# Ten of twenty zeroing transfers move from the GpSimd queue to the sync queue

## The chip, the cores and the metric

The kernel runs on one NeuronCore of one Trainium2 chip. The metric is the device time of one execution in microseconds (us); the kernel before has a median of 4244.83 us over three runs (4243.64 to 4254.43).

## The reference

Two layers of a graph network over 6250 nodes of width 256 and 106250 edges, sorted by destination, each followed by a residual and a layer norm.

```python
edge_index = jnp.stack([src, dst])
# layer 0: a message per edge, summed over the edges of node ei
hi, hj = h[ei], h[ej]
x = jnp.concatenate((hi, hj, d2), axis=-1)
msg = silu(x @ mW1 + mb1)
msg = layer_norm(msg, ln_g, ln_b)
msg = silu(msg @ mW2 + mb2)
agg = segment_sum(msg, ei, num_segments=6250)
y = silu(concatenate((h, agg)) @ uW1 + ub1) @ uW2 + ub2
x = layernorm(x + (h + y))
# layer 1: gather, mean by node, one linear layer
agg = segment_sum(x[src], dst) / maximum(counts, 1)
x = layernorm(x + relu(agg @ W.T + b))
```

## The kernel before

The 6250 nodes are 50 blocks of 125. The edges are 832 tiles of 128, handled four at a time: 208 quads (and 220 quads of "visits", since a tile that lies over two blocks is visited twice). The first matrix of the message is applied to the nodes, not to the edges, so that an edge's input is a sum of two rows: one of a table P in HBM (`p_tab`), gathered by the edge's index, and one of a table Q that stays in SBUF (`big`), spread over the edges by a one-hot matmul.

The stages, in the times of the profile:

- 0 to about 142 us: P is computed block by block and stored, while the index tables are made. SP issues the stores (line 480), the two tables of places and edge weights (lines 460, 462), and other transfers.
- 142 to about 195 us: Q is computed (line 787 on TensorE, 1013 and 1016 on ScalarE, 1419 and 1423 on VectorE). On GpSimd the gathers of P begin at 148 us (`gather_0`, line 628). The ring in SBUF (`ring0`) holds 16 quads of gathered rows.
- From 202 us the expansion: for each quad v SP loads its places (line 450, 125 KB from `loc_tab`) and its weights (line 452, 3 KB) in `place_rows(v)`; VectorE makes the one-hot matrix of it (line 1445); TensorE multiplies it with Q (line 836); VectorE adds the product onto the gathered rows (line 1464). The places have two buffers, so `place_rows(v)` waits on SP for the expansion of quad v-2 (semaphore `qexp`). On VectorE the order is: add quad v, one-hot of quad v+2, add quad v+1. The expansion runs 14 quads ahead of the message: the first SiLU (line 1034, ScalarE) waits until quads 0 to 13 are added.
- From 282 to 2896 us the messages: SiLU, norm, second matrix, SiLU, and a matmul that joins edges of a tile with the same node. Then GpSimd adds the 128 rows of each tile onto one of four tables of sums in HBM (`sums`, line 639, an accumulating indirect DMA). GpSimd gathers quad g+16 only once the SiLU of quad g has read its place in the ring (line 625), and adds quad q once ScalarE has written its sums (line 634). After the 16 gathers that fill the ring, each quad costs GpSimd four gathers and four adds.
- 2896 to 3092 us: the nodes of layer 0 (the four tables are read, added and multiplied). From 3092 us on: layer 1, with gathers of its own.

The four tables of sums, 6400 rows each, must be zero before the first add. `zero_piece(eng, i)` (line 397, its DMA at line 401) writes one fifth of one table: 1280 KB from an SBUF tile of zeros, which is `scr`, the tile that VectorE's `count_before` (line 1509) writes later, and so waits for all twenty pieces (line 1504). In the kernel before GpSimd issues all twenty: pieces 0 to 9 during the P stage, each after five more blocks, and pieces 10 to 19 one behind each of the first ten quads of gathers (line 648). `weight_rows(part)` on SP (line 468) copies weight rows into Q; part 2 waits for the last matmul of Q (`s_qmm`), and TensorE's first expansion waits for it (line 869).

The order on every queue is the order of the code: each engine's block is written out, and SP's `message_loop` (line 491) comes right after `weight_rows(2)`.

Of the kernel before, what the change touches and what calls it, by code (L numbers as in the profile page):

```python
# [27 lines left out]
BLOCKS = N // NB  # L28
# [5 lines left out]
TABLES = QT  # L34
# [4 lines left out]
XGROUP = 5  # L39
# [8 lines left out]
LAG = -(-BEHIND // QT) + 1  # L48
# [5 lines left out]
def gnn(nc, x, src, dst, edge_w, mW1, mb1, ln_g, ln_b, mW2, mb2, uW1, ub1, uW2, ub2, W, b, out):  # L54
# [13 lines left out]
    with ExitStack() as ctx:  # L68
        def sb(name, shape, dt=f32):
            return ctx.enter_context(nc.sbuf_tensor(name, shape, dt))  # L70

        def sem(name):
            return ctx.enter_context(nc.semaphore(name))
# [36 lines left out]
        cnt = sb("cnt", [NB, 2, BLOCKS])  # L110
# [8 lines left out]
        def cut(shape, dt=f32, parts=P):  # L119

            n = 1
            for m in shape:
                n *= m
            words = n if dt != bf16 else n // 2
            ap = arena[:, at_[0]:at_[0] + words]
            at_[0] += words
            assert at_[0] <= at_[1], at_
            ap = ap if dt == f32 else ap.bitcast(dt)
            names = "abcd"[:len(shape)]
            ap = ap.rearrange(f"p ({' '.join(names)}) -> p {' '.join(names)}", **dict(zip(names, shape)))  # L130
            return ap[0:parts]
# [47 lines left out]
        half = cut([2, 2, D])  # L179
        agg = cut([2, D])  # L180
        col = cut([2, 2 * H, P])
        xin = cut([2, D])
        hpre = cut([2, D])
        hpre2 = cut([2, D])
        hid = cut([2, D])
# [23 lines left out]
        mom = sb("mom", [P, 2, 5, QT])  # L209
# [34 lines left out]
        def by_place(rows_, group):  # L244
# [2 lines left out]


        s_const, s_constc, s_zeroed, s_pad = sem("s_const"), sem("s_constc"), sem("s_zeroed"), sem("s_pad")
        s_edges, s_weights, s_tables = sem("s_edges"), sem("s_weights"), sem("s_tables")  # L250
        s_ends, s_tile, s_prev, s_range = sem("s_ends"), sem("s_tile"), sem("s_prev"), sem("s_range")
        s_epart, s_blk, s_pick, s_picked, s_visit = (sem("s_epart"), sem("s_blk"), sem("s_pick"), sem("s_picked"),
                                                     sem("s_visit"))
# [24 lines left out]
                ["hot", "agg", "acc"]]  # L278
        e = [{n: sem(f"e{l}_{n}") for n in EDGE[l]} for l in range(2)]

        BLOCK = ["load0", "load1", "xcopy", "half", "agg", "cnt", "cols", "colev", "hmm", "hpre", "hid", "hcols", "hcolev",
                 "omm", "oadd", "res", "stat", "mom", "newt", "norm"]
        k = [{n: sem(f"b{l}_{n}") for n in BLOCK} for l in range(2)]
        s_scaled, s_lastnorm = sem("s_scaled"), sem("s_lastnorm")
        s_mean, s_biased, s_shift = sem("s_mean"), sem("s_biased"), sem("s_shift")
        s_norm1 = {n: sem(f"s_norm1_{n}") for n in ("dve", "act")}
# [77 lines left out]
        def later(q, n):  # L364

            return not isinstance(q, int) or q >= n
# [24 lines left out]
        def load_x(eng, g):  # L391
            rows_ = x[g * XGROUP * NB:(g + 1) * XGROUP * NB, :].rearrange("(j p) d -> p j d", p=NB)
            for a, z in SPLIT:
                eng.dma_start(pxin[a:z, g % 2, :, :], rows_[a:z]).then_inc(s_xload[g % 2], 16)
        ZPIECES = 5

        def zero_piece(eng, i):
            rows_ = SUMROWS // P * D // ZW
            n, a = rows_ // ZPIECES, i % ZPIECES * (rows_ // ZPIECES)
            whole = sums[i // ZPIECES].rearrange("(p a b) d -> p a (b d)", p=P, a=rows_)  # L400
            eng.dma_start(whole[:, a:a + n, :], zeros[:, :].unsqueeze(1).to_broadcast([P, n, ZW]))\
                .then_inc(s_tables, 16)

        def visit_blocks(eng, q, regs):

# [10 lines left out]
        def _(sp):  # L416
# [47 lines left out]
            def weight_rows(part):  # L464
                a, z, done = W_PARTS[part]
                if done:
                    sp.wait_ge(s_qmm, done)
                sp.dma_start(big[NB:P, a:z, :, :].rearrange("p j k d -> p j (k d)"),
                             w1cp[0:PARTS, :, :].rearrange("p k d -> p (k d)").unsqueeze(1)
                             .to_broadcast([PARTS, z - a, PARTS * D])).then_inc(s_wrow, 16)  # L470
# [12 lines left out]
                place_rows(v, v)  # L483
            for part in range(1, len(W_PARTS)):
                weight_rows(part)


            def step_0(q, k_):
# [70 lines left out]
        def _(pool):  # L559
# [46 lines left out]
                    pool.sem_inc(s_turn_pool, 1)  # L606
                    place(c)

            EARLY = BLOCKS // XGROUP
            for i in range(EARLY):  # L610
                pool.wait_ge(s_xt, XGROUP * (i + 1))
                zero_piece(pool, i)
            pool.wait_ge(s_padrows, 16 * 2)
            for par in (0, 1):
                pool.wait_ge(s_pst[par], 32 * ((BLOCKS // PAIR + 1 - par) // 2))
# [5 lines left out]
            def gather_0(g):  # L621
                if g >= RING_QUADS + 4:
                    pool.wait_ge(e[0]["pre"], QT * (g - 3))
                if g >= RING_QUADS:
                    pool.wait_ge(e[0]["silu"], 2 * (g - RING_QUADS + 1))
                for u in range(QT):
                    tile = g * QT + u
                    pool.indirect_dma_start(  # L628
                        out=ring0[:, tile % RING, :], out_offset=None, in_=p_tab[:, :],
                        in_offset=bass.IndirectOffsetOnAxis(ap=esrc[:, tile:tile + 1], axis=0))\  # L630
                        .then_inc(landed(g)[0], 16)

            def add(q, par):
                pool.wait_ge(e[0]["tot"], q + 1)
                pool.wait_ge(e[0]["sidx"], q + 1)
                for u in range(QT):
                    if q >= 1:
                        pool.wait_ge(e[0][f"added{u}"], q * 16)
                    pool.indirect_dma_start(  # L639
                        out=sums[u][:, :], in_=tot[:, par, u, :], in_offset=None,  # L640
                        out_offset=bass.IndirectOffsetOnAxis(ap=sidx[:, par, u:u + 1], axis=0),
                        compute_op=ALU.add).then_inc(e[0][f"added{u}"], 16)

            for q in range(-LAG - 1, TILE_QUADS + 2):
                if q + LAG + 1 < TILE_QUADS:
                    gather_0(q + LAG + 1)
                if q + LAG + 1 < TABLES * ZPIECES - EARLY:
                    zero_piece(pool, EARLY + q + LAG + 1)
                if q == 2:
                    pool.wait_ge(s_tables, 16 * TABLES * ZPIECES)  # L650
                if q >= 2:
                    add(q - 2, q % 2)

# [8 lines left out]
                                      .rearrange("p a d -> p (a d)")).then_inc(k[0]["xcopy"], 1)  # L662
            steps(pool, BLOCKS, 0, copy_x)
            pool.wait_ge(s_x1st, STORES)
            pool.wait_ge(s_tables, 16 * TABLES * ZPIECES)
            pool.wait_ge(s_esrc, 1)
            for tile in range(TILE_QUADS * QT):

# [503 lines left out]
        def _(dve):  # L1172
# [327 lines left out]
            def count_before(q, par, u):  # L1500

                if u == 0:
                    if isinstance(q, int) and q == 0:
                        dve.wait_ge(s_tables, 16 * TABLES * ZPIECES)
                        dve.wait_ge(s_padrows, 16 * 2)
                    dve.wait_ge(s["same"], q + 1)
                    if later(q, 1):
                        dve.wait_ge(s["dup"], QT * q)
                nc.vector.tensor_tensor_reduce(out=scr[:, u, :], in0=same[:, par, u, :], in1=lower[:, :],
                                               scale=1.0, scalar=0.0, op0=ALU.mult, op1=ALU.add,  # L1510
                                               accum_out=dup[:, par, u:u + 1]).then_inc(s["dup"], 1)
# [21 lines left out]
            def step_0(q, k_):  # L1533
                par = k_ % 2
                o = 1 - par

                def beside(i):
                    if live(q - 1, TILE_QUADS):
                        if i == 0:
                            sum_rows(q - 1, o, 0)  # L1540
                        elif i == 1:
                            count_before(q - 1, o, 0)
                            count_before(q - 1, o, 1)
                        elif 8 < i <= 10:
                            count_before(q - 1, o, i - 7)
                        elif i == 12:
                            sum_rows(q - 1, o, 1)
                        elif i == 14:
                            sum_rows(q - 1, o, 2)
                    if live(q + LAG + 2, QUADS) and i == 4:  # L1550
                        one_hot(q + LAG + 2, (k_ + LAG) % 2)
                if live(q + LAG, QUADS):
                    add_in(q + LAG, (k_ + LAG) % 4)
                if live(q, TILE_QUADS):
                    stage_keys(q, par)
                    norm(q, par, beside)
                else:
                    for i in range(5 + 2 + 3 * NEWTON):
                        beside(i)
# [207 lines left out]
```

## Time and profile before

| what | value |
|---|---|
| median of three runs | 4244.83 us (4243.64 to 4254.43) |
| span of the profiled execution, first to last instruction | 4447.1 us |
| busy share of the span: TensorE, VectorE, ScalarE, GpSimd | 73%, 61%, 34%, 68% |
| DMA queue q0 (software, GpSimd's) | 353.53 MB, 41.7% of 16 engines |
| DMA queue q1 (hardware, SP's) | 93.80 MB, 7.4% |
| granted TensorE clock, mean | 0.858 |

The span is the profiled execution's own time as far as the profile gives it: 202 us longer than the median of the runs that were timed without a profile. Of an instruction on a DMA-issuing queue a row tells when it was issued and how long the issue took; when its bytes landed is told apart.

### The profile page before, as it was taken

Reading aid. Unit: us, or ns where it says so; the run is one execution under the profiler, and the core shown is the slowest. Engines: PE = TensorE matmul, PEld = TensorE weight load, DVE = VectorE, ACT = ScalarE, POOL = GpSimd, SP = SyncE. Lnnn points to the kernel's source line nnn. Section 1 sums busy time; section 2 is a strip of 40 time slices with the busy share of each in tenths; the row PEclk is TensorE's granted clock in tenths of the full one; section 3 lists DMA queues with packets and bytes.
Section 4 is the critical chain, followed back from the end, with each engine's and each line's share of the span. In section 5 each row is a group of like instructions: output and inputs, shape, how many; then the busy total and the mean of one; then the engine's idle time right before and its main releaser. Section 6 shows DMA issues by size and latency. Waiting matters only on the chain. (4 is left out here: it accounts for less than half of the span.)

```text
span 4447.1 us, 77452 instructions
## 1 busy us (share of the span) xinstructions
PE 3267.0 (73%) x16199; PEld 2413.6 (54%) x16200; DVE 2708.1 (61%) x12039; ACT 1491.9 (34%) x2782; POOL 3024.4 (68%) x2641
## 2 busy tenths in 40 slices
PE   6757777777777777777777778887476766667676
PEld 4446666566666666665666666675243433334345
DVE  5456666666666666666666667777344444444457
ACT  1324444444544444444444445633000000000005
POOL 1538888888888888888888887612666666666643
PEclk9878998889899899899998989998777777777788
DMA  6725555555555555555555555755333333333323
GB/s 194 257 67 93 93 94 94 93 94 95 93 93 94 94 92 94 94 93 93 94 94 92 94 94 85 132 158 161 90 92 90 90 90 92 90 91 91 90 61 113
DMA packets 315268, 455.28 MB, mean 102 GB/s; under 512 B 51945, under 2 KB 255301, under 8 KB 314949
## 3 DMA queue, kind: packets, MB, share of 16 engines
q0 software_dynamic: 206400, 353.53, 41.7%
q1 hardware_dynamic: 103317, 93.80, 7.4%
q10 hardware_dynamic: 5232, 5.12, 0.4%
q14 instruction: 293, 2.40, 0.2%
q8 instruction: 26, 0.43, 0.0%
HBM read 296.41 MB, written 155.62 MB: 102 GB/s over the span
## 5 line engine op out<-in xcount | busy, mean ns | idle before, releaser
L639 POOL DMA_INDIRECT sum<-arena,sidx x832 | 1321.3, 1588 | 294.2 <-issue 254.1
L671 POOL DMA_INDIRECT arena<-x_tab,esrc x832 | 796.5, 957 | 436.9 <-issue 188.7
L945 PE MATMUL ps<-arena 128*125 x1760 | 711.4, 494 | 444.5 <-DVE arena L1703 217.8
L628 POOL DMA_INDIRECT arena<-p_tab,esrc x832 | 820.7, 986 | 309.5 <-issue 246.5
L812 PE MATMUL ps<-arena 128*128 128x256 f32 x1664 | 560.5, 496 | 444.5 <-ACT arena L1062 442.7
L849 PE MATMUL ps<-w,arena 128*128 128x256 f32 x3328 | 833.6, 383 | 3.9 <-ACT arena L1072 3.9
L945 PEld LDWEIGHTS ps<-arena 128*125 128x125 f32 x1760 | 392.6, 241 | 744.0 <-issue 681.9
L1703 DVE TENSOR_TENSOR arena<-ps,arena 125x257 f32 x880 | 374.7, 426 | 647.7 <-remote 219.5
L812 PEld LDWEIGHTS ps<-arena 128*128 128x128 f32 x1664 | 389.9, 246 | 550.3 <-issue 485.1
L849 PEld LDWEIGHTS ps<-w,arena 128*128 128x128 f32 x3328 | 567.4, 190 | 121.0 <-issue 4.7
L1464 DVE TENSOR_TENSOR arena<-ps,arena 128x256 f32 x880 | 373.0, 424 | 381.5 <-issue 197.8
L1044 ACT ACTIVATE arena<-ps,key 128x128 f32<-128x128 f32 x832 | 237.8, 369 | 1090.1 <-remote 1076.9
L836 PE MATMUL ps<-arena 128*128 x2640 | 411.6, 317 | 53.3 <-DVE arena L1464 27.0
L1473 DVE BATCH_NORM_STATS2 bst<-arena 128x6 f32<-128x256 f32 x832 | 312.4, 417 | 226.9 <-ACT arena L1034 224.2
L1144 ACT ACTIVATE arena<-ps 128x250 f32<-128x250 f32 x50 | 18.8, 376 | 1250.6 <-PE ps L965 1249.5
L836 PEld LDWEIGHTS ps<-arena 128*128 128x128 bf16 x2640 | 304.5, 115 | 174.2 <-issue 86.2
L949 PE MATMUL ps<-identh 128*128 128x512 bf16 x832 | 387.9, 466 | 0.0
L1496 DVE TENSOR_SCALAR arena<-arena,mom,nwt 128x256 f32<-128x256 f32 x832 | 313.0, 437 | 37.1 <-DVE nwt L387 30.2
L822 PE MATMUL ps<-ident,arena 128*128 128x128 f32 x1664 | 225.9, 279 | 132.8 <-DVE arena L1496 90.5
L1055 ACT ACTIVATE arena<-ps,gb 128x512 f32<-128x512 f32 x416 | 320.4, 770 | 8.2 <-PE ps L822 6.0
L822 PEld LDWEIGHTS ps<-ident,arena 128*128 128x128 f32 x1664 | 185.4, 143 | 188.4 <-DVE arena L1496 93.7
L1072 ACT ACTIVATE arena<-ps 128x1024 f32<-128x1024 f32 x208 | 213.1, 1024 | 166.3 <-PE ps L812 76.5
(189 smaller groups left out, 4049.1 us busy)
## 6 DMA issues: line engine op xcount, KB each, us to landing
arena<-loc_tab SPq DMA_DIRECT2D x220, 125.0 KB
sum<-scr POOLq DMA_DIRECT2D x20, 1280.0 KB
arena<-sum SPq DMA_DIRECT2D x200, 128.0 KB, 2.2
arena<-p_tab,esrc POOLq DMA_INDIRECT x832
sum<-arena,sidx POOLq DMA_INDIRECT x832
arena<-x_tab,esrc POOLq DMA_INDIRECT x832
arena<-x_tab SPq DMA_DIRECT2D x50, 128.0 KB, 2.0
p_tab<-arena SPq DMA_DIRECT2D x25, 224.0 KB
```

The source lines that it names most:

```text
L628: pool.indirect_dma_start(out=ring0[:, tile % RING, :], out_offset=None, in_=p_tab[:, :], in_offset=bass.IndirectOffsetOnAxis(ap=esrc[:, t ...
L639: pool.indirect_dma_start(out=sums[u][:, :], in_=tot[:, par, u, :], in_offset=None, out_offset=bass.IndirectOffsetOnAxis(ap=sidx[:, par, u ...
L671: pool.indirect_dma_start(out=ring[:, tile % LATER_RING, 0:D], out_offset=None, in_=x1_tab[:, :], in_offset=bass.IndirectOffsetOnAxis(ap=e ...
L812: last = nc.tensor.matmul(ps[:, PM + u // 2, u % 2 * D:(u % 2 + 1) * D], same[:, par, u, :], msg[:, par, u, 0:D], start=True, stop=True)
L822: last = nc.tensor.transpose(ps[:, PZ + h, u * P:(u + 1) * P], act[:, par, u, h * P:(h + 1) * P], ident[:, :])
L836: last = nc.tensor.matmul(ps[:, PP + u // 2, u % 2 * D:(u % 2 + 1) * D], hott[:, par, u, :], big[:, bass.ds(blocks_[u], 1), i, :].rearrang ...
L849: nc.tensor.matmul(to, zt[:, par, h, u * P:(u + 1) * P], w2[:, h, :], start=h == 0, stop=False)
L945: nc.tensor.matmul(ps[0:NB, u, 0:CW], same1[:, par, u, :], ring[:, bass.ds(at[u], 1), :].rearrange("p a c -> p (a c)"), start=True, stop=T ...
L949: nc.tensor.matmul(ps[:, PK, :], identh[:, :], identh[:, :].unsqueeze(1).to_broadcast([P, QT, P]), start=True, stop=True)
L1055: nc.scalar.activation(zt[:, par, h, :], ps[:, PZ + h, :], ACT.Identity, bias=gb[:, h, 1:2], scale=gb[:, h, 0:1]).then_inc(s["zev"], 1)
L1464: nc.vector.tensor_tensor(row, ps[:, PP + u // 2, u % 2 * D:(u % 2 + 1) * D], row, ALU.add)\
L1703: nc.vector.tensor_tensor(row, ps[0:NB, u, 0:CW], row, ALU.add).then_inc(s["acc"], 1)
```

## The change

SP issues pieces 10 to 19, in one run after `weight_rows(2)` and ahead of its message loop, on a semaphore of their own (`s_later`). GpSimd no longer issues them between gathers. The waits for zeroed tables now ask both semaphores, and GpSimd's second wait, ahead of the gathers of layer 1, is left out. Some semaphores that nothing used are no longer made.

```diff
+        EARLY = BLOCKS // XGROUP
-        def zero_piece(eng, i):
+        def zero_piece(eng, i, zeroed):
...
-                .then_inc(s_tables, 16)
+                .then_inc(zeroed, 16)
...
             for part in range(1, len(W_PARTS)):
                 weight_rows(part)
+            for i in range(EARLY, TABLES * ZPIECES):
+                zero_piece(sp, i, s_later)
...
             for q in range(-LAG - 1, TILE_QUADS + 2):
                 if q + LAG + 1 < TILE_QUADS:
                     gather_0(q + LAG + 1)
-                if q + LAG + 1 < TABLES * ZPIECES - EARLY:
-                    zero_piece(pool, EARLY + q + LAG + 1)
                 if q == 2:
-                    pool.wait_ge(s_tables, 16 * TABLES * ZPIECES)
+                    pool.wait_ge(s_tables, 16 * EARLY)
+                    pool.wait_ge(s_later, 16 * (TABLES * ZPIECES - EARLY))
...
             pool.wait_ge(s_x1st, STORES)
-            pool.wait_ge(s_tables, 16 * TABLES * ZPIECES)
...
-                        dve.wait_ge(s_tables, 16 * TABLES * ZPIECES)
+                        dve.wait_ge(s_tables, 16 * EARLY)
+                        dve.wait_ge(s_later, 16 * (TABLES * ZPIECES - EARLY))
```

## Rows read from the trace of the kernel before

**Rows 1.** The waits of the whole span: who waited for whom, total, times, longest.
```profile
POOL sum L639 <- issue: 254.1, 802, 6.6
POOL arena L628 <- issue: 246.5, 809, 0.3
POOL arena L628 <- ACT arena L1034: 49.8, 2, 45.1
```
**Rows 2.** Timeline of GpSimd: start, duration, engine, line, operation, idle time before.
```profile
148.47 1.15 POOL L628 DMA_INDIRECT arena<-p_tab,esrc  x1 [7.08 <-DMA p_tab<-arena]
...
153.65 0.92 POOL L401 DMA_DIRECT2D sum<-scr  x1
...
208.75 0.92 POOL L401 DMA_DIRECT2D sum<-scr  x1
...
237.56 0.95 POOL L628 DMA_INDIRECT arena<-p_tab,esrc  x1 [0.30 <-issue]
238.81 0.95 POOL L628 DMA_INDIRECT arena<-p_tab,esrc  x1 [0.30 <-issue]
284.85 0.95 POOL L628 DMA_INDIRECT arena<-p_tab,esrc  x1 [45.09 <-ACT arena L1034]
...
305.75 1.64 POOL L639 DMA_INDIRECT sum<-arena,sidx  x1 [6.60 <-issue]
```
**Rows 3.** Timeline of ScalarE: the table load ahead of the first SiLU.
```profile
282.14 1.28 ACT L1034 ACT_TABLE_LOAD   x1 [87.10 <-DVE arena L1464]
```
**Rows 4.** Timeline of VectorE during the expansion of the first quads.
```profile
212.20 0.35 DVE L1445 TENSOR_SCALAR arena<-arena,tnum 125x512 bf16<-125x512 bf16 x1 [5.75 <-DMA arena<-loc_tab]
...
220.98 0.35 DVE L1445 TENSOR_SCALAR arena<-arena,tnum 125x512 bf16<-125x512 bf16 x1 [2.58 <-issue]
224.23 0.42 DVE L1464 TENSOR_TENSOR arena<-ps,arena 128x256 f32 x1 [2.90 <-issue]
...
237.47 0.42 DVE L1464 TENSOR_TENSOR arena<-ps,arena 128x256 f32 x1 [12.24 <-remote]
...
243.95 0.42 DVE L1464 TENSOR_TENSOR arena<-ps,arena 128x256 f32 x1 [2.88 <-remote]
...
247.15 0.35 DVE L1445 TENSOR_SCALAR arena<-arena,tnum 125x512 bf16<-125x512 bf16 x1 [0.96 <-DMA arena<-loc_tab]
...
278.93 0.35 DVE L1445 TENSOR_SCALAR arena<-arena,tnum 125x512 bf16<-125x512 bf16 x1 [1.85 <-PE ps L836]
```
**Rows 5.** Timeline of SP's queue, from the last two weight row copies on.
```profile
168.14 26.38 SPq L468 DMA_DIRECT2D arena<-arena  x2
205.28 0.28 SPq L450 DMA_DIRECT2D arena<-loc_tab  x1
```
**Rows 6.** Windows: busy us of each engine, granted clock, DMA share, GB/s.
```profile
180.00:190.00 10.00, 9.66 (x41) 6.40 (x40) 7.38 (x20) 6.58 (x21) 7.87 (x9) 1.00 0.93 325
195.00:215.00 20.00, 5.25 (x27) 3.33 (x28) 4.28 (x11) 0.04 (x1) 15.74 (x17) 0.61 0.93 303
230.00:240.00 10.00, 1.38 (x6) 0.77 (x6) 0.85 (x2) 0.00 (x0) 7.59 (x8) 0.50 0.40 114
```
**Rows 7.** DMA issues of the page: size of each.
```profile
arena<-loc_tab SPq DMA_DIRECT2D x220, 125.0 KB
sum<-scr POOLq DMA_DIRECT2D x20, 1280.0 KB
```
**Rows 8.** Timeline of SP's queue late in layer 1: a store, then small loads.
```profile
4391.70 1.04 SPq L513 DMA_DIRECT2D out_dram<-arena  x2
4392.78 19.69 SPq L543 DMA_DIRECT2D arena<-x_tab  x10
```
**Rows 9.** Line 543 from 4392 to 4396 us, then the page's row of such loads.
```profile
DMA to landing us min/median/max: 6.3/6.3/6.3
...
arena<-x_tab SPq DMA_DIRECT2D x50, 128.0 KB, 2.0
```
**Rows 10.** SP's queue as it loads x, and the DMA queues from 2842 to 2845 us.
```profile
2839.74 27.39 SPq L496 DMA_DIRECT2D arena<-in_x_dram  x10
...
q1 hardware_dynamic: 847, 0.87, 108.6%
```

More of the change, by code:

```diff
@@ L249, in gnn @@
         s_const, s_constc, s_zeroed, s_pad = sem("s_const"), sem("s_constc"), sem("s_zeroed"), sem("s_pad")
-        s_edges, s_weights, s_tables = sem("s_edges"), sem("s_weights"), sem("s_tables")
+        s_edges, s_weights, s_tables, s_later = sem("s_edges"), sem("s_weights"), sem("s_tables"), sem("s_later")
         s_ends, s_tile, s_prev, s_range = sem("s_ends"), sem("s_tile"), sem("s_prev"), sem("s_range")
@@ L279, in gnn @@
         e = [{n: sem(f"e{l}_{n}") for n in EDGE[l]} for l in range(2)]
-        BLOCK = ["load0", "load1", "xcopy", "half", "agg", "cnt", "cols", "colev", "hmm", "hpre", "hid", "hcols", "hcolev",
-                 "omm", "oadd", "res", "stat", "mom", "newt", "norm"]
-        k = [{n: sem(f"b{l}_{n}") for n in BLOCK} for l in range(2)]
+        BLOCK = [["load0", "load1", "xcopy", "half", "agg", "cols", "colev", "hmm", "hpre", "hid", "hcols", "hcolev",
+                  "omm", "oadd", "res", "stat", "mom", "newt", "norm"],
+                 ["load0", "load1", "cnt", "cols", "colev", "omm", "res", "stat", "mom", "newt"]]
+        k = [{n: sem(f"b{l}_{n}") for n in BLOCK[l]} for l in range(2)]
         s_scaled, s_lastnorm = sem("s_scaled"), sem("s_lastnorm")
@@ L607, in _ @@
                     place(c)
-            EARLY = BLOCKS // XGROUP
             for i in range(EARLY):
                 pool.wait_ge(s_xt, XGROUP * (i + 1))
-                zero_piece(pool, i)
+                zero_piece(pool, i, s_tables)
             pool.wait_ge(s_padrows, 16 * 2)
```

## The prediction

> **What bounds the kernel now.** I read the total waits first. From the first add on, GpSimd waits for almost nothing but its own issue: 254.1 us of 0.3 us gaps before adds, 246.5 us before gathers, and one long wait of 45.1 us, for the first SiLU [rows 1]. So over most of the span, 306 to 2896 us, GpSimd sets the pace, and what happens before moves the end only as far as it moves the moment at which that chain starts: the first SiLU at 282.14 us [rows 3], after which the seventeenth quad is gathered at 284.85 and the first add is issued at 305.75 [rows 2]. Second, the timelines from 148 us to there. GpSimd fills its ring by 239.8 and then stands idle for 45.09 us [rows 2]; it is early. ScalarE had waited 87.10 us for VectorE's adds [rows 3]. The late chain is the expansion: places from SP's queue, one-hot, matmul, add, quad by quad [rows 4]. It starts when part 2 of the weight rows has landed and then needs the places of quads 2 to 13. VectorE's one-hot of quad 2 comes at 212.20, released by that small load, which SP issued at 205.28 [rows 4, 5]: 6.9 us for 125 KB, at a time at which the DMA engines were 0.93 busy at 303 GB/s [rows 6].
>
> **The change part by part.**
>
> GpSimd loses ten issues of 0.92 us, the first at 153.65, the last at 208.75 [rows 2]: 9.2 us. Its ring would be full at 230.6 rather than 239.8. What hides this gain is the 45.09 us of waiting right behind it, so it is worth nothing; it would be worth 9.2 us only if the first SiLU came before GpSimd was done.
>
> SP gains ten issues at 194.5, where the last weight row copy ends (168.14 + 26.38) [rows 5]. All of SP's later instructions stand behind them: place_rows(2), (3) and all that follow, and so VectorE's one-hot of quad 2, everything behind that on VectorE in order (the add of quad 1, the one-hot of quad 3), TensorE's expansion of quad 2 and the first SiLU. Quads 0 and 1 are not touched; their places were loaded before.
>
> What these ten cost in the queue is not shown by the trace of before for these transfers, but a close case is: near the end SP issues a store of 1250 KB in two parts at 4391.70, and right behind it two loads of 128 KB [rows 8]. These two land after 6.3 us; the median of such loads is 2.0 [rows 9]. The extra 4.3 us is the store's own duration, 1.28 MB at 298 GB/s. A small transfer on SP's queue lands after the large one ahead of it. The load of x shows that SP itself is held back too: ten issues, 6.25 MB, take it 27.39 us [rows 10].
>
> So the places of quad 2 land when the ten pieces have. Ten times 1280 KB is 13.1 MB [rows 7]. Beside them run the gathers that are left. A gather starts every 1.25 us [rows 2], so a quad takes 5.0 us and, from 148.5 on, 9.2 quads are out by 194.5; 6.8 quads of 512 KB (128 rows of 1 KB, four times) remain, 3.6 MB. Together 16.7 MB at the 303 GB/s of [rows 6] take 55.1 us: until 249.6, and with the 2.0 us of a small load [rows 9] the one-hot of quad 2 comes at 251.6 and not at 212.2. That is 39.4 us later. The lower end is 13.1 MB alone at 325 GB/s, the best rate of [rows 6]: 40.3 us, the one-hot at 236.8, 24.6 us later. The upper end is all bytes at the 260 GB/s that I allow for 1 KB packets beside other traffic, worked out as 0.9 of the 289 GB/s at which SP's queue alone moved 0.87 MB in 3 us [rows 10]: 64 us, the one-hot at 260.7, 48.5 us later. I take the middle value, since 303 GB/s is for a mix of just these transfers.
>
> How much of the 39.4 us reaches the first SiLU? Before, there are 69.9 us from the one-hot of quad 2 (212.20) to 282.14. Much of it is the chain itself: from the one-hot of quad 6 (247.15) to that of quad 14 (278.93) a quad takes 3.97 us [rows 4]. But three gaps in it are no part of the chain: 2.90, 12.24 and 2.88 us before adds at 224.23, 237.47 and 243.95, for which the profile names no engine [rows 4]. They are 18.0 us and stand just after the DMA engines had been saturated. If they come from that load, they are not repeated: at 252 us the zeroing and the gathers are both over. Then the first SiLU is at 251.6 + 69.9 - 18.0 = 303.5, 21.4 us later than before. If they belong to that place in the code, they return, and the shift is the full 39.4 us. With all three gaps gone and the lower end of the queueing, the shift is 24.6 - 18.0 = 6.6 us; with them back and the upper end, 48.5 us. I take 21.4, because nothing of the sort appears in the later quads [rows 4], which run without load.
>
> Less DMA load between 148 and 194 us makes part 2 of the weight rows land sooner (by up to some 5 us, as their wait was about 8 us under load against 2.0 for a small load without it). This is worth nothing here, as quads 0 and 1 then only wait for quad 2. It would be worth 5 us if SP's queue were not blocked.
>
> VectorE's and GpSimd's waits for zeroed tables: the pieces are landed by about 250 us, the first use of the tile of zeros comes after the first SiLU, 303 us. No cost, with 50 us of cover; it would cost if the pieces took over 100 us. The added second wait is one more instruction. The wait that is left out ahead of layer 1 was long met. The semaphores no longer made cost nothing at run time.
>
> After that nothing gives the time back. A quad costs GpSimd 12.6 us in the long stage (four gathers at 1.25, four adds at 1.9), on 208 quads, and it starts later by the same amount. The sum is 0 (GpSimd) + 21.4 (expansion) = 21.4 us. It is made within a span of 4447.1 us; the timed runs are 202 us shorter, mostly, I think, because each of GpSimd's issues is a little quicker without the profiler, and the transfers, which make up this sum, should take the same. So I add it unscaled to the median: 4244.8 + 21.4 = 4266.
>
> A rule speaks against my view and for the change. The Trainium skill, page "DMA: Bandwidth & Descriptors", section "SWDGE vs HWDGE vs iDMA", has it that plain transfers belong on SP or ScalarE, whose descriptors are made in hardware, and that GpSimd is to be kept for irregular ones. By that rule GpSimd is relieved and the 9.2 us above are won. The trace agrees with its premise (0.92 us of GpSimd for each piece [rows 2]) and not with the gain, as GpSimd idles for 45 us behind them.
>
> **The rivals.**
>
> One: the halts return. The mechanism is the same, and the shift is 39.4 us: 4284. For it speaks that no engine is named for them, so that load is only my guess, and that, if the profiler caused them, the timed runs of before never had them. Against it: they stand where the load was.
>
> Two: SP's queue does not hold the places back, because the DMA engines take packets of both transfers by turns. Then the first expansion starts some 5 us sooner, the one-hot of quad 2 no longer waits 5.75 us, and the kernel is faster by about 8 us: 4237; if the halts go as well, by 26: 4219. It decides at the one-hot of quad 2: if it comes before 212, the change wins. For it speaks that GpSimd's ten issues are gone and its load is spread less tightly; against it the 6.3 us of [rows 9], in one and the same queue.
>
> Three: no change. The queue is blocked, but only until about 237, and the halts vanish: the shift is 6.6 us, 4251. For it speaks the best rate of 325 GB/s; against it that the gathers run beside the zeroing until 229.
>
> **How the numbers follow.** Forecast 4266: 0.52. The halts return, 4284: 0.30. SP's queue does not block: 0.07, of which 0.05 are faster by over 0.3% and 0.02 within it. The short block: 0.11, within 0.3%. I call 0.3% (12.7 us) what a measurement of this kernel can tell from no change. So slower 0.82, same 0.13, faster 0.05. The likeliest case alone has 4258 to 4275. The range reaches down to the short block, 4250, and up to the halts with the slow rate, 4292.
>
> **What would show it.** GpSimd's first 64 gathers run without a gap until about 230, and then it waits for the first SiLU not 45 but some 75 us (21 for the shift, 9 for the issues). SP shows ten issues from about 194.5, of which the later ones take several us each, and the places of quad 2 right behind them, about 245. The one-hot of quad 2 stands at about 252, released by the load of the places. DMA is over 0.9 busy from 197 to 250 and light from 155 to 194. The first SiLU is near 303, the first add near 327, and each later stage is later by the same. I am wrong if the one-hot of quad 2 comes before 225, or if the shift at the first add is not found at the end.

## The result, and the profile after

The changed kernel takes 4276.44 us (median of four runs, 4272.4 to 4278.52) against 4246.65 us for the kernel before (four runs, 4243.64 to 4254.43): ratio 1.0074, 95% interval 1.0062 to 1.0086. A second comparison, with after_again below, gave 1.0084 (1.0070 to 1.0097). The change costs 30 to 36 us. The forecast was 4266, range 4250 to 4292.

SP's queue in the changed kernel, in order of time (start, duration of the issue):

```profile
192.48 0.77 SPq L470 DMA_DIRECT2D arena<-arena  x1
193.30 38.21 SPq L403 DMA_DIRECT2D sum<-scr  x10
231.56 3.24 SPq L452 DMA_DIRECT2D arena<-loc_tab  x1
234.84 2.22 SPq L454 DMA_DIRECT2D arena<-wgt_tab  x1
237.11 0.99 SPq L452 DMA_DIRECT2D arena<-loc_tab  x1
```

The ten issues hold SP for 38.21 us, and the load of the places of quad 2, issued at 205.28 before [rows 5], is issued at 231.56. The row of line 403 alone, from 190 to 232 us, gives the duration of one issue (in ns) and the time from issue to landing (in us), each as min, median and max:

```profile
L403 SPq DMA_DIRECT2D sum<-scr x10: 427/4587/5186, 193.3 to 226.5; - x10
...
DMA to landing us min/median/max: 9.2/16.4/18.2
```

A piece lands up to 18.2 us after it was issued. So the queue holds pieces that SP is already rid of, and the places stand behind these as well: issued at 231.56, used at 244.05. VectorE, ScalarE and GpSimd, three timelines, answer to [rows 4], [rows 3] and [rows 2]:

```profile
244.05 0.35 DVE L1446 TENSOR_SCALAR arena<-arena,tnum 125x512 bf16<-125x512 bf16 x1 [40.57 <-DMA arena<-loc_tab]
```
```profile
294.76 1.28 ACT L1035 ACT_TABLE_LOAD   x1 [100.98 <-DVE arena L1465]
```
```profile
228.12 0.94 POOL L631 DMA_INDIRECT arena<-p_tab,esrc  x1 [0.30 <-issue]
297.47 0.94 POOL L631 DMA_INDIRECT arena<-p_tab,esrc  x1 [68.41 <-ACT arena L1035]
...
319.15 1.63 POOL L642 DMA_INDIRECT sum<-arena,sidx  x1 [7.19 <-ACT arena L1073]
```

VectorE waits 40.57 us for one 125 KB load. GpSimd has filled its ring by 229 and then idles 68.41 us. The windows of the changed kernel (busy us of the engines, then granted clock, DMA share and GB/s) answer to [rows 6]:

```profile
150.00:190.00 40.00, 39.51 (x157) 26.07 (x156) 29.26 (x78) 26.68 (x78) 30.54 (x32) 1.00 0.38 106
195.00:235.00 40.00, 4.91 (x24) 3.13 (x24) 1.70 (x4) 0.00 (x0) 25.84 (x28) 0.57 1.04 387
```

The DMA engines are 0.38 busy while Q is computed, and at their full share (1.04) when the expansion should begin; TensorE is busy for 4.91 of the 40 us.

The profile of before that stands ahead of the prediction belongs to an unusual execution: its span was 4447.1 us, at a mean granted clock of 0.858. Why that execution took longer is open. The span of the profile after is 4276.8 us, as long as the timed runs. The first experiment profiles the kernel before anew, and the two kernels are compared by that.

### The profile page after: what moved, and what is told of

Read it like the earlier page. It is cut to its first block, busy times and chain, and to the rows that moved or that the text cites. A ratio compares the mean times of both kernels' runs of the same rounds, so it can differ in the third digit from the quotient of the medians.

```text
span 4276.8 us, 77454 instructions
## 1 busy us (share of the span) xinstructions
PE 3213.0 (75%) x16199; PEld 2374.0 (56%) x16200; DVE 2672.6 (62%) x12039; ACT 1537.5 (36%) x2782; POOL 3000.5 (70%) x2631
## 4 chain that ended last, share of the span: by engine, by line
POOL 36%; PE 21%; issue 20%; DMA 14%; DVE 5%; SPq 2%; ACT 1%; DVEq 1%; ACTq 0%; POOLq 0%
POOL sum L642 20%; POOL arena L631 14%; PE ps L946 9%; DMA arena<-x_tab,esrc 9%; DMA sum<-arena,sidx 3%; PE ps L950 3%; POOL arena L672 2%; PE ps L900 2%; PE ps L813 1%; PE ps L850 1%; PE ps L788 1%; DMA p_tab<-arena 1%; PE ps L837 1%; SPq L403 1%; PE ps L918 1%
## 5 line engine op out<-in xcount | busy, mean ns | idle before, releaser
L946 PE MATMUL ps<-arena 128*125 x1760 | 665.8, 466 | 326.6 <-DMA arena<-x_tab,esrc 277.7
L946 PEld LDWEIGHTS ps<-arena 128*125 128x125 f32 x1760 | 380.9, 227 | 589.0 <-issue 505.6
L823 PE MATMUL ps<-ident,arena 128*128 128x128 f32 x1664 | 268.4, 313 | 466.1 <-DVE arena L1497 466.1
L813 PE MATMUL ps<-arena 128*128 128x256 f32 x1664 | 519.4, 469 | 3.4 <-ACT arena L1063 3.3
L837 PE MATMUL ps<-arena 128*128 x2640 | 396.9, 291 | 162.0 <-DVE arena L1465 152.5
L823 PEld LDWEIGHTS ps<-ident,arena 128*128 128x128 f32 x1664 | 209.3, 158 | 544.6 <-DVE arena L1497 403.1
L837 PEld LDWEIGHTS ps<-arena 128*128 128x128 bf16 x2640 | 268.1, 102 | 316.7 <-issue 241.7
L950 PE MATMUL ps<-identh 128*128 128x512 bf16 x832 | 378.4, 455 | 0.0
L1497 DVE TENSOR_SCALAR arena<-arena,mom,nwt 128x256 f32<-128x256 f32 x832 | 300.5, 423 | 7.7 <-DVE nwt L388 0.2
```

Source lines behind the costliest of these rows:

```text
L813: last = nc.tensor.matmul(ps[:, PM + u // 2, u % 2 * D:(u % 2 + 1) * D], same[:, par, u, :], msg[:, par, u, 0:D], start=True, stop=True)
L823: last = nc.tensor.transpose(ps[:, PZ + h, u * P:(u + 1) * P], act[:, par, u, h * P:(h + 1) * P], ident[:, :])
L837: last = nc.tensor.matmul(ps[:, PP + u // 2, u % 2 * D:(u % 2 + 1) * D], hott[:, par, u, :], big[:, bass.ds(blocks_[u], 1), i, :].rearrang ...
L946: nc.tensor.matmul(ps[0:NB, u, 0:CW], same1[:, par, u, :], ring[:, bass.ds(at[u], 1), :].rearrange("p a c -> p (a c)"), start=True, stop=T ...
L950: nc.tensor.matmul(ps[:, PK, :], identh[:, :], identh[:, :].unsqueeze(1).to_broadcast([P, QT, P]), start=True, stop=True)
```

## The experiments

Line numbers differ by up to three between kernels: line 403 is the zeroing, 452 (450 before) the load of places, 1446 (1445) the one-hot, 1035 (1034) the SiLU.

**b_again: the kernel before, without an edit.**

> The kernel before once more, for a second profile. Theory Q (queue): the change costs what the ten pieces hold back the places of quad 2 on SP's queue, 31.9 us (one-hot of quad 2 at 212.2 before, 244.05 after), and all of it reaches the end, since the three gaps of 18.0 us without a named engine belonged to that one profiled execution and not to the kernel. Then this profile has no such gaps, the first SiLU comes at about 264 us and not at 282, and the layer 1 stage takes about 1178 us as in the profile of after, not 1355. Theory G (gaps are the kernel's): the gaps are there again, the SiLU at about 282, and 18 us of the slowdown come from somewhere later. Time as before, within 0.1%, for both.

Measured: 4246.25 us, ratio 1.0004 (0.9995 to 1.0013), span 4242.4. VectorE's one-hots of quads 2 and 4, ScalarE's table load, GpSimd's first add:

```profile
213.22 0.35 DVE L1445 TENSOR_SCALAR arena<-arena,tnum 125x512 bf16<-125x512 bf16 x1 [6.30 <-DMA arena<-loc_tab]
...
222.20 0.58 DVE L1445 TENSOR_SCALAR arena<-arena,tnum 125x512 bf16<-125x512 bf16 x1 [2.86 <-DMA arena<-loc_tab]
```
```profile
266.61 1.28 ACT L1034 ACT_TABLE_LOAD   x1 [71.07 <-DVE arena L1464]
```
```profile
269.32 0.94 POOL L628 DMA_INDIRECT arena<-p_tab,esrc  x1 [29.15 <-ACT arena L1034]
...
290.98 1.75 POOL L639 DMA_INDIRECT sum<-arena,sidx  x1 [7.86 <-issue]
```

The one-hot of quad 2 is where it was but for 1.0 us [rows 4], while the first SiLU comes at 266.61, not at 282.14 [rows 3]. Between 150 and 290 us VectorE's longest wait for which no engine is named is 0.62 us. From the first gather of layer 1 (3066.31) to the end are 1176 us; the first profile had 1354 (from 3092.78), the changed kernel has 1178 (from 3098.86). The three gaps of 18.0 us and the 178 us of layer 1 belonged to that one execution. Against b_again the first SiLU of the changed kernel is 28.15 us later and its first add 28.17 us.

**sp_early: the ten pieces ahead of weight_rows(1).**

```diff
             for v in range(2):
                 place_rows(v, v)
+            for i in range(EARLY, TABLES * ZPIECES):
+                zero_piece(sp, i, s_later)
             for part in range(1, len(W_PARTS)):
                 weight_rows(part)
-            for i in range(EARLY, TABLES * ZPIECES):
-                zero_piece(sp, i, s_later)
```

> The changed kernel with SP's ten pieces issued ahead of weight_rows(1), right after the places of quads 0 and 1, at about 147 us, where the DMA engines are 0.36 busy in the changed kernel. Theory Q: 13.1 MB beside the gathers are through at about 190, part 2 of the weight rows lands as fast as after (first expansion at about 199.5), the places of quad 2 wait for nothing, its one-hot comes at about 205, 7 us sooner than before the change: about 4239 us, ratio to before 0.998. Theory L (load, not queue: moving 13.1 MB by SP costs wherever it stands, as hardware descriptors take the engines from the gathers): the gathers of the first quads land late and the time stays above before, 4255 or more.

Measured: 4241.11 us beside 4246.35, ratio 0.9989 (0.9980 to 0.9998).

```profile
146.43 33.99 SPq L403 DMA_DIRECT2D sum<-scr  x10
180.47 13.42 SPq L470 DMA_DIRECT2D arena<-arena  x2
204.13 0.31 SPq L452 DMA_DIRECT2D arena<-loc_tab  x1
```
```profile
207.50 0.37 DVE L1446 TENSOR_SCALAR arena<-arena,tnum 125x512 bf16<-125x512 bf16 x1 [2.21 <-DMA arena<-loc_tab]
```
```profile
259.12 1.28 ACT L1035 ACT_TABLE_LOAD   x1 [64.72 <-DVE arena L1465]
```

The same bytes from the same queue, 47 us sooner, cost nothing: TensorE and VectorE are at work on Q in that stretch, and the time is not above that of before. The first SiLU is 7.5 us sooner than in b_again. It is not the hardware queue as such that is slow. This run also keeps every other edit of the change (the two semaphores, the wait left out, the semaphores no longer made), so these don't cost the 30 us either.

**act_late: the ten pieces from ScalarE's queue, at the time of the change.**

```diff
-            for i in range(EARLY, TABLES * ZPIECES):
-                zero_piece(sp, i, s_later)
...
             for q in range(BLOCKS + 1):
                 q_step(q, q % 2)
+            for i in range(EARLY, TABLES * ZPIECES):
+                zero_piece(ac, i, s_later)
```

> The changed kernel with the ten pieces issued by ScalarE's queue, after its last copy of Q, at the same moment as SP did (about 194 us): the same bytes at the same time, in another queue. Theory Q: SP's small loads no longer stand behind them; they take some 7 us each under load and not 3, the one-hot of quad 2 comes at 206 to 213: between 4238 and 4250 us, ratio 0.998 to 1.001. Theory L (the load of the DMA engines at this moment delays the places, whichever queue it is in): one-hot of quad 2 past 230, 4265 us or more.

Measured: 4262.65 us beside 4246.35, ratio 1.0037 (1.0023 to 1.0051): neither theory's number. SP's queue, then VectorE's one-hots of quads 2, 4 and 6, then ScalarE:

```profile
219.65 0.27 SPq L452 DMA_DIRECT2D arena<-loc_tab  x1
```
```profile
213.63 0.35 DVE L1446 TENSOR_SCALAR arena<-arena,tnum 125x512 bf16<-125x512 bf16 x1 [8.61 <-DMA arena<-loc_tab]
...
229.93 0.35 DVE L1446 TENSOR_SCALAR arena<-arena,tnum 125x512 bf16<-125x512 bf16 x1 [7.57 <-DMA arena<-loc_tab]
...
243.84 0.35 DVE L1446 TENSOR_SCALAR arena<-arena,tnum 125x512 bf16<-125x512 bf16 x1 [5.77 <-DMA arena<-loc_tab]
```
```profile
279.34 1.28 ACT L1035 ACT_TABLE_LOAD   x1 [84.13 <-DVE arena L1465]
```

The one-hot of quad 2 is at 213.63, as in b_again: the block is gone, and this part of theory Q holds. ScalarE's ten issues end at 236.3, long before its first SiLU, so it isn't ScalarE that is late. But the loads on SP's free queue are slow while the pieces from the other queue keep the engines at a share of 1.04: the places of quad 4, issued at 219.65, are used at 229.93, 10.3 us later; in b_again they are issued at 218.21 and used at 222.20, 4.0 us later. The first SiLU is 12.7 us later than in b_again. VectorE's waits up to it account for that: 29.9 us in all for places (20.0 in b_again) and 6.7 ahead of adds with no engine named (4.0). So a queue of their own for the ten pieces would spare 15.4 of the 28.15 us, and 12.7 would stay.

**half: five pieces early, five where the change has ten.**

```diff
+            for i in range(EARLY, EARLY + 5):
+                zero_piece(sp, i, s_later)
             for part in range(1, len(W_PARTS)):
                 weight_rows(part)
-            for i in range(EARLY, TABLES * ZPIECES):
+            for i in range(EARLY + 5, TABLES * ZPIECES):
                 zero_piece(sp, i, s_later)
```

> The changed kernel with five of SP's pieces issued early (ahead of weight_rows(1)) and five where the change has all ten. Theory Q: the blocked time is proportional to the bytes ahead; the ten took from 193.3 to about 240, so five end at about 216 to 217, and the one-hot of quad 2 comes at about 220: 8 us later than before, 4255 us, ratio 1.002. A rival in which SP's issue itself (a full ring) or one fixed stall costs the 31 us would give the same as ten pieces, 4276.

Measured: 4257.64 us beside 4246.35, ratio 1.0028 (1.0016 to 1.0041).

```profile
223.15 0.35 DVE L1448 TENSOR_SCALAR arena<-arena,tnum 125x512 bf16<-125x512 bf16 x1 [19.25 <-DMA arena<-loc_tab]
```

None, five and ten pieces behind weight_rows(2) put the one-hot of quad 2 at 207.50 (sp_early), 223.15 and 244.05, and the first SiLU at 259.12, 274.33 and 294.76: the first SiLU is later by 15.2 us with the first five and by 20.4 with the second. The expectation had the one-hot at 220. The delay grows with the pieces ahead, and one fixed stall is ruled out; whether it goes by their bytes or by their number isn't told apart, as all pieces are alike.

**sp_mid: the ten pieces between the two weight row copies.**

```diff
-            for part in range(1, len(W_PARTS)):
-                weight_rows(part)
+            weight_rows(1)
             for i in range(EARLY, TABLES * ZPIECES):
                 zero_piece(sp, i, s_later)
+            weight_rows(2)
```

> The changed kernel with SP's ten pieces between weight_rows(1) and weight_rows(2), so issued from about 168 us on. Now it is part 2 of the weight rows that stands behind them, and with it the first expansion, while the places of quad 2 are free. Theory Q (a transfer waits for the bytes ahead of it on SP's queue): 13.1 MB at the 0.29 to 0.34 MB per us of after and sp_early end at about 205 to 209; part 2 lands some 7 us later, the first expansion comes at about 213 (202.99 in b_again, 201.36 in sp_early) and the one-hot of quad 2 at about 218, 5 us later than in b_again: 4251 us, ratio 1.001. If it were the places alone that the pieces hurt, this would be as fast as sp_early, 4241.

Measured: 4267.82 us beside 4248.64, ratio 1.0045 (1.0031 to 1.0059). The direction was right and the size was not. SP, then TensorE's first expansion:

```profile
168.32 38.03 SPq L403 DMA_DIRECT2D sum<-scr  x10
206.40 4.90 SPq L470 DMA_DIRECT2D arena<-arena  x1
```
```profile
225.13 1.24 PE L837 MATMUL ps<-arena 128*128 x5 [32.06 <-DMA arena<-arena]
```

The weight rows landed at about 225, not at 213: I had taken the end of SP's issues for the end of the transfers, while the queue still held pieces. Places that are free do not help if another small transfer is blocked: 76.5 KB of weight rows hold up the first expansion by 22 us (202.99 in b_again).

**interleave: one piece behind each of ten loads of places.**

```diff
-            for i in range(EARLY, TABLES * ZPIECES):
-                zero_piece(sp, i, s_later)
...
                     place_rows(q + LAG + 2, (k_ + LAG) % 2)
+                    if isinstance(q, int) and q + LAG < TABLES * ZPIECES - EARLY:
+                        zero_piece(sp, EARLY + q + LAG, s_later)
```

> The changed kernel with SP's ten pieces spread: one behind each of the loads of the places of quads 2 to 11. No small load then stands behind more than one piece, 1.31 MB, 3.4 to 4.4 us. Theory Q: the one-hot of quad 2 comes at about 207; after it each loop over two quads (8 us) is longer by up to 3.5 us while the pieces last, so 17 us in all at most, the first SiLU at 260 to 277 (b_again 266.6, after 294.8), 4241 to 4257 us. Theory L (what counts is the load during the expansion, not the order in the queue): about as act_late, SiLU at 279, 4262 us.

Measured: 4257.86 us beside 4248.64, ratio 1.0019 (1.0010 to 1.0028).

```profile
270.92 1.28 ACT L1035 ACT_TABLE_LOAD   x1 [76.12 <-DVE arena L1465]
```

The first SiLU is 4.3 us later than in b_again, within the range expected by theory Q (260 to 277); the time is 0.9 us above its upper edge. Spreading the same ten pieces on the same queue, from 203.4 to 251.4 us, saves 23.8 of the 28.15 us at the first SiLU.

**pool_after: the ten pieces from GpSimd, once the ring is full.**

```diff
-            for i in range(EARLY, TABLES * ZPIECES):
-                zero_piece(sp, i, s_later)
...
+                if q + LAG + 1 == RING_QUADS - 1:
+                    for i in range(EARLY, TABLES * ZPIECES):
+                        zero_piece(pool, i, s_later)
```

> The changed kernel with the ten pieces back on GpSimd, but behind the sixteen gathers that fill the ring, in the time in which it waits for the first SiLU anyway (from about 228 us). SP's queue holds only small loads. The nine us of issue are hidden. Theory Q alone: the places are never blocked, as fast as sp_early, 4241 us. With the load effect that act_late showed (small loads of 5 to 8 us and not 3 while the engines are saturated, 12.7 us later at the first SiLU for 45 us of load): the load is 34 to 40 us long here, from 230 on, so the SiLU comes some 10 us later than in sp_early, at 266 to 271, 4246 to 4251 us.

Measured: 4265.89 us beside 4248.64, ratio 1.0036 (1.0022 to 1.0050), above both expectations.

```profile
235.87 0.49 DVE L1447 TENSOR_SCALAR arena<-arena,tnum 125x512 bf16<-125x512 bf16 x1
...
247.80 0.35 DVE L1447 TENSOR_SCALAR arena<-arena,tnum 125x512 bf16<-125x512 bf16 x1 [8.32 <-DMA arena<-loc_tab]
```
```profile
275.78 1.28 ACT L1036 ACT_TABLE_LOAD   x1 [81.68 <-DVE arena L1466]
```

GpSimd's time is free here, the engines' is not: the first SiLU is 16.7 us later than in sp_early, where I expected 10. The load effect of act_late is there again, on SP's otherwise empty queue: the places of quad 10, issued at 237.58, are used at 247.80, 10.2 us later. The window of 230 to 260 us holds almost nothing but pieces issued by GpSimd one behind the other:

```profile
230.00:260.00 30.00, 10.95 (x48) 6.46 (x48) 8.55 (x20) 0.00 (x0) 8.00 (x10) 0.54 1.00 374
```

GpSimd's queue too moves 374 GB/s when the pieces follow each other without gathers between.

**sp_early_again: sp_early once more.**

> The kernel of sp_early once more, to narrow its interval, which was 0.998 to 0.9998: 4241 us, ratio 0.999 again, since its first add came 7.6 us sooner than in b_again; a ratio of 1.000 would say that the gain was noise.

Measured: 4246.22 us beside 4248.64, ratio 0.9994 (0.9985 to 1.0003). First SiLU at 261.14, 5.5 us sooner than in b_again. Both times the ratio was below one; its interval excludes 1 only in the first. The gain over the kernel before is 0.1% in the first run, 0.06% in the second, and not shown by the second alone. The gain over the changed kernel is certain: 0.9989 against 1.0074.

**b_third and after_again: both kernels once more, without an edit.**

> The kernel before a third time, beside after_again. The first add came at 290.98 us in b_again and the first gather of layer 1 2775.3 us behind it; in the six changed kernels this distance was 2776.2 to 2786.5. If it is a property of the kernel before, it is 2775 here again; if it scatters from run to run, up to 2780. No gaps without a named engine, the first SiLU at 265 to 268 and layer 1 at 1175 to 1180 us, as theory Q has it.

> The changed kernel once more, for its ratio on the same chip as b_third and a second profile. Theory Q: one-hot of quad 2 at 243 to 246, first add at 318 to 321, 28 us later than in b_third, and the timed difference 28 to 33 us (ratio 1.0066 to 1.0078). The distance from the first add to layer 1 was 2779.7: again, or down to 2775 if it was scatter; then the timed difference is 28.

Measured: the kernel before (b_third) 4246.59 us, ratio 1.0004 (0.9995 to 1.0013), first SiLU 265.01, first add 289.72, first gather of layer 1 at 3068.34. The changed kernel (after_again) 4279.86 us, ratio 1.0084 (1.0070 to 1.0097), above the 1.0066 to 1.0078 expected, one-hot of quad 2 at 243.88, first SiLU 294.48, first add 318.18, layer 1 at 3099.05. The first add is 28.5 us later and layer 1 30.7 us. From the first add to layer 1 there are 2775.3 and 2778.6 us in the two new profiles of before and 2779.7 and 2780.9 in those of after: it scatters, but the changed kernel had 1 to 6 us more in every pairing.

The kernels side by side (times in us; the first three columns are from one profile each, the last is the difference of the medians of one comparison):

| kernel | one-hot of quad 2 | first SiLU | first add | time less before |
|---|---|---|---|---|
| b_again | 213.22 | 266.61 | 290.98 | -0.1 |
| the change | 244.05 | 294.76 | 319.15 | +29.8 |
| sp_mid | 231.34 | 282.56 | 306.44 | +19.2 |
| pool_after | 205.34 | 275.78 | 299.85 | +17.3 |
| act_late | 213.63 | 279.34 | 302.38 | +16.3 |
| half | 223.15 | 274.33 | 299.10 | +11.3 |
| interleave | 206.64 | 270.92 | 295.17 | +9.2 |
| sp_early | 207.50 | 259.12 | 283.37 | -5.2 |
| sp_early_again | 209.26 | 261.14 | 284.19 | -2.4 |

In all eight rows with the change in some form the end moved more than the first add: by 1.6 to 8.4 us against the profile of b_again, by 0.4 to 7.1 against that of b_third. That is small beside the scatter of one kernel's runs, but has one sign, in sp_early too, where nothing is blocked. Whether it belongs to the other edits of the change or to the later stages, no run here tells.

## Why the prediction came out as it did

**GpSimd's saving hidden: right.** Its ring was full by 229 (forecast about 230), and its wait grew to 68.41 us. The forecast was 75, reckoned from a wait of 45.09 that was 29.15 in b_again; the growth was 39.3 us against b_again and not 30.

**The places stand behind the ten pieces: right.** VectorE waited 40.57 us for them. That more pieces ahead make it later is shown by half. That it is their place in SP's queue which blocks the load is shown by act_late, where the one-hot of quad 2 is at 213.63 with the same pieces in another queue. Most of the block is SP itself being held: against b_again the load is issued 25.8 us later (231.56 and 205.76), and then takes 5.0 us longer until it is used (12.5 and 7.5).

**The size of the block: 39.4 us forecast, 30.8 measured** (213.22 to 244.05). The term that was mis-sized is the rate. I took 303 GB/s from [rows 6] for what the engines can do; the changed kernel moved 387. My own figures could have warned me: GpSimd issued one piece and one quad of gathers, 1.83 MB, every 6.1 us [rows 2], which is 300 GB/s. So that window very likely showed GpSimd's pace of issue, and not what the engines can move, although their share was 0.93; pool_after, where the same queue moved 374 GB/s, speaks for it. The landing behind the pieces was mis-sized the other way. At 387 GB/s from 194.5 on, and with my 2.0 us for the small load, the sum gives 239.7, 4.3 us too early: from 235 to 240 the engines moved only 237 GB/s, at a mean share of 0.63, and the load issued at 231.56 was used 12.5 us later. (The 6.25 MB that I gave for the load of x are 6.4 MB; nothing in the sum hangs on it.)

**The three gaps: this step failed.** I put them down to the DMA load before them and credited the change with 18.0 us, which made 39.4 into 21.4. They were no part of the kernel at all: b_again has none, nor has b_third (longest 0.79 us). The rival with 39.4 us named this case ("if the profiler caused them, the timed runs of before never had them"). The same mistake stands in my reading of the span: I put 202 us more than the median down to the profiler's cost for each issue, while the new profiles have spans of 4242.4 and 4248.1 us. The two errors, 8.6 us too much and 18.0 too little, partly cancelled, so that 4266 lies 10 us below the measured 4276.44. That is luck in part: with the block at its true size and my credit for the gaps the forecast would have been 4258, 19 us too low, and with my size of the block but no credit for the gaps it would have been 4284, 8 us too high: the first rival, which lies nearer than my likeliest case.

**From the one-hot to the SiLU: right.** 51.9 us without the gaps; 53.4 and 52.0 in the two new profiles of before, 50.7 and 50.6 in those of the changed kernel.

**All of it reaches the end: right in kind.** The first add moved by 28.17 and 28.46 us in the two pairs, the start of layer 1 by 32.55 and 30.71, the time by 29.8 us in the medians, and by ratio by 31 and 36. The remaining few us arise behind the first add or scatter there; where is open. It is largest in pool_after, 8 us more at the end than at the first add, which is not explained either.

**The cause, as the runs leave it.** In the changed kernel it is the queue, as forecast: the whole shift stands ahead of the one-hot of quad 2 (30.8 us in the first pair, 30.9 in the second), and from there to the first SiLU the changed kernel is 1.4 to 2.7 us quicker than before, since its pieces are over by then. What the forecast did not see is what remains without the block. With the same pieces in ScalarE's queue the first SiLU is still 12.7 us later than in b_again, because the DMA load then falls on the chain of small loads. So 15.4 of the 28.15 us go if the pieces leave SP's queue but keep their time, 23.8 if they stay in it but are spread, and all if they go to the stretch of Q. The split is that of these placements; others would split it otherwise.

**GpSimd relieved: worth nothing, as forecast.** The 9.2 us were not to be had here. The rule of the Trainium skill that the prediction weighed (page "DMA: Bandwidth & Descriptors", section "SWDGE vs HWDGE vs iDMA") gives plain transfers to SP or ScalarE. Read as a gain of 9.2 us it fails in this kernel, which is 30 us slower, and the measurement decides; that SP can issue these pieces at no cost is shown by sp_early. What sp_early gained at the first SiLU (7.5 and 5.5 us) goes with an earlier one-hot of quad 2 (207.50 and 209.26 against 213.22), and isn't GpSimd's, which waits 33.33 us for the first SiLU there.

## What to carry to other kernels

What these runs suggest: a large transfer that nothing needs soon belongs where nothing waits for a small one, that is, not ahead of a small load in its queue, and not beside a chain that lives on the latency of such loads, even from another queue. Look for a stretch in which the compute engines are busy and need no transfer; the same ten pieces cost 30 us or nothing by where they stood. If there is none, spread them: one piece behind each small load cost 9 us. Before taking a gap or a rate from a profile, compare its span with the timed median, and ask whether a measured rate is that of the engines or of whoever issues.

## What the runs showed of the hardware

- With SP's pieces and GpSimd's gathers together the DMA engines moved 387 GB/s from 195 to 235 us (397 in sp_early from 150 to 180), where the same zeroing from GpSimd, between its gathers, moved 303 from 195 to 215 us (293 in b_again) at a busy share of 0.93. GpSimd's pieces one behind the other moved 374 (pool_after, 230 to 260), so it isn't GpSimd's queue that is slower. A busy share of 0.93 did not mean that nothing more could be moved.
- SP's issue returns before the bytes are moved, in the changed kernel: a piece of 1280 KB took a median of 4.59 us to issue and landed 9.2 to 18.2 us after the issue. The end of a run of issues is not the end of its transfers, and a small load behind them lands last: issued at 231.56, used at 244.05.
- A 125 KB load issued while another queue keeps the engines at a share of 1.0 is used 10 us after its issue (10.3 in act_late, 10.2 in pool_after). Beside GpSimd's pieces and gathers at 0.96 it is 7.5 us (b_again, quad 2), after them at 0.66 it is 4.0 (quad 4), and beside gathers alone 3.4 (sp_early, quad 2).
